# A new order of the calls on all engines in a fused mixture and three transformer blocks, and another last reader of one bank

## What is computed

```python
x_norm = modulate(_ln(x), shift_a, scale_a)
q, k, v = split(x_norm @ W_qkv + b_qkv)               # 16 heads of 16
attn_w = softmax(einsum('bhqd,bhkd->bhqk', q, k) * scale)
x = x + gate_a * (heads(attn_w @ v) @ W_proj + b_proj)
q_c = _ln(x) @ W_qc + b_qc
k_c, v_c = split(_ln(context) @ W_kvc + b_kvc)         # 77 context tokens
x = x + heads(softmax(q_c @ k_c * scale) @ v_c) @ W_cproj + b_cproj
h = gelu(modulate(_ln(x), shift_m, scale_m) @ W_mlp1 + b_mlp1)   # 1024 wide
x = x + gate_m * (h @ W_mlp2 + b_mlp2)
```

## Time and profile before

| | |
|---|---|
| median of 3 runs | 2887.1 us |
| the profiled execution | 2888.95 us, span 2887.1 us |
| busy: TensorE, VectorE, ScalarE, GpSimd | 94%, 64%, 54%, 33% |
| mean granted clock of TensorE | 0.974 |
| TensorE busy, 850 to 2810 us | 1873.45 of 1960 us |
| spread of the reciprocals, first to last unit | 733 to 2814 us, 47 units' distance |

### The profile page before, as it was taken

How to read it: one execution, slowest core, us unless ns; L and a number is a source line. 1 busy time by engine, 2 the same in 40 slices (tenths; PEclk the granted TensorE clock), 3 DMA queues, 4 the chain that set the end, 5 groups by cost and what they waited for, 6 DMA issues and landing times.

```text
span 2887.1 us, 64022 instructions
## 1 busy us (share of the span) xinstructions
PE 2716.0 (94%) x24276; PEld 2292.3 (79%) x24276; DVE 1834.0 (64%) x3776; ACT 1554.4 (54%) x2715; POOL 949.1 (33%) x963
## 2 busy tenths in 40 slices
PE   7999999994899999999999999999999999999998
PEld 6999999993577777777777777777777778778776
DVE  2444444434667777777677777777676676776753
ACT  3444444432365656655555566556555665665653
POOL 3444444321123333333232332332333223333223
PEclk9999999996799999999999999999999999999998
DMA  5123222105244453454455544434445445445331
GB/s 158 63 93 102 90 82 91 51 9 159 66 101 98 102 120 91 101 115 104 121 121 134 115 92 109 117 88 108 120 108 145 117 105 115 92 103 109 90 79 42
DMA packets 280418, 290.63 MB, mean 101 GB/s; under 512 B 90736, under 2 KB 206816, under 8 KB 280112
## 3 DMA queue, kind: packets, MB, share of 16 engines
q1 hardware_dynamic: 268656, 259.65, 36.7%
q10 hardware_dynamic: 11456, 26.88, 3.0%
HBM read 105.33 MB, written 35.85 MB: 49 GB/s over the span
## 4 chain that ended last, share of the span: by engine, by line
PE 58%; DVE 6%; issue 5%; POOL 2%; DMA 2%; SPq 2%; ACT 1%; ACTq 0%; POOLq 0%; DVEq 0%
PE gbank L3394 9%; PE obank L3234 8%; PE obank L3241 6%; PE gbank L3234 6%; PE obank L3319 5%; PE score L3299 4%; PE obank L3365 3%; PE score L3285 3%; DVE m_a L2596 2%; PE score L3348 2%; PE gbank L3249 2%; PE gbank L3334 2%; PE obank L3334 2%; PE gbank L3225 2%; PE obank L3468 1%
## 5 line engine op out<-in xcount | busy, mean ns | idle before, releaser
L2049 ACT ACTIVATE p_f<-score 128x1024 f32<-128x1024 f32 (+1 forms) x576 | 566.9, 1022 | 243.2 <-PE score L3299 219.3
L2596 DVE TENSOR_REDUCE m_a<-score 128x4 f32<-128x1024 f32 x384 | 459.4, 1218 | 132.6 <-PE score L3285 132.3
L1897 POOL TENSOR_TENSOR h_c<-h_f,h_c 128x512 fp32r<-128x512 f32 x192 | 246.4, 1284 | 640.5 <-DVE h_c L2670 640.5
L3394 PE MATMUL gbank<-w_down,h_c 128*128 128x256 f32 x2304 | 336.5, 294 | 1.2 <-POOL h_c L1897 1.2
L3394 PEld LDWEIGHTS gbank<-w_down,h_c 128*128 128x128 f32 x2304 | 292.4, 190 | 16.0 <-POOL h_c L1897 1.6
L1153 PE MATMUL m_ps<-m_comb,m_w 128*128 128x256 f32 x2304 | 295.4, 284 | 1.5 <-PEq L253 1.5
L1153 PEld LDWEIGHTS m_ps<-m_comb,m_w 128*128 128x128 f32 x2304 | 279.9, 188 | 5.0 <-issue 3.6
L2606 DVE TENSOR_REDUCE m_b<-gbank 128x4 f32<-128x308 f32 x192 | 92.1, 480 | 224.5 <-PE gbank L3334 191.7
L768 POOL TENSOR_TENSOR m_hhl<-m_hf,m_hhl 128x512 fp32r<-128x512 f32 x96 | 125.1, 1303 | 267.2 <-DVE m_hhl L992 267.2
L3319 PE MATMUL obank<-p_f,v_s 128*20 128x256 f32 x3072 | 204.2, 396 | 0.5 <-ACT p_f L2049 0.4
L3299 PE MATMUL score<-q_cat,k_cat 50*128 50x256 f32 x1536 | 190.3, 318 | 9.7 <-DMA q_cat<-mT_a 7.9
(11 more groups left out here) (289 smaller groups left out, 5613.6 us busy)
## 6 DMA issues: line engine op xcount, KB each, us to landing
q_cat<-q_hl SPq DMA_DIRECT2D x288, 128.0 KB, 3.5
k_cat<-k_hl SPq DMA_DIRECT2D x288, 128.0 KB, 3.8
qc_cat<-qc_hl SPq DMA_DIRECT2D x288, 128.0 KB, 3.1
split_L<-m_cut SPq DMA_DIRECT2D x36, 512.0 KB, 4.1
x_a<-x_after_L SPq DMA_DIRECT2D x48, 256.0 KB, 2.6
x_b<-x_after_L SPq DMA_DIRECT2D x48, 256.0 KB, 4.2
kc_cat<-kc_hl SPq DMA_DIRECT2D x288, 39.0 KB, 2.0
x_after_L<-y_c SPq DMA_DIRECT2D x32, 256.0 KB, 2.4
```

The source lines that it names most:

```text
L1897: e.tensor_tensor(h_c[:, 1, 2 * i:2 * i + 2, :], h_f[:, i % 2, :, :], h_c[:, 0, 2 * i:2 * i + 2, :].bitcast(F32), ALU.subtract).then_inc(S ...
L2049: e.activation(p_f[i % 4][0:n, :], score[i % 2].ap[0:n, :, :].rearrange("p h n -> p (h n)"), ACT.Exp, scale=SCALE).then_inc(ex.sem, 1)
L2596: e.tensor_reduce(m_a[:, :, i::NPAIR].rearrange("p t h -> p h t"), score[i % 2].ap[:, :, :].rearrange("p h (t k) -> p h t k", t=TT), AX.X, ...
L3394: mm = e.matmul(B_DOWN.ap[:, tt, :], h_c[:, xp, 2 * i + c, tt * P:(tt + 1) * P], W["down"][:, i, wp, c, :], start=(i + wp + xp + c == 0), ...
```

## The change

1. All five lists of calls are put in another order. Each list holds the same calls as before; the start and the end that are written out become longer (the loops run over n = 10 to 41, 11 to 41 or 11 to 42 instead of 5, 6 or 7 to 44 or 46). The `next_...` calls outside of the loops, where they did nothing, are gone.
2. On VectorE `cross_values_out` comes ahead of `cross_keys_low`. The bank that both read is given back by the later of them, so the wait in `cross_keys_values` that leaves the signal changes.

```diff
@@ cross_keys_values
                 e.wait_ge(*S["K_cT"].at(a))
-                turn(B_KV, S["K_vs"], a)
+                turn(B_KV, S["K_kl"], a)
```

The loop of TensorE after, from the reciprocals on, one turn (indices as in the loop over n):

```diff
+                self_recips_spread(n - 3)
+                cross_keys_values(n - 3)
+                self_projected(n - 3)
+                up(n - 5, 2)
+                self_plain(n - 2, 7)
...
+                self_turned(n - 2)
+                up(n - 6, 3)
+                self_max_rows(n - 3)
+                cross_turned(n - 4)
+                keys(n - 2)
+                cross_queries(n - 4)
+                cross_recips_spread(n - 5)
+                queries(n - 2)
+                self_scores(n - 3, 0)
+                self_scores(n - 3, 1)
+                down(n - 6, 0)
+                down(n - 6, 1)
+                down(n - 6, 2)
+                cross_projected(n - 5)
+                down(n - 6, 3)
+                self_scores(n - 3, 2)
+                self_scores(n - 3, 3)
+                cross_plain(n - 4, 0, 0)
+                cross_plain(n - 4, 0, 1)
+                self_values(n - 3, 0)
...
+                cross_plain(n - 4, 2, 1)
+                down(n - 6, 4)
+                self_scores(n - 3, 6)
+                cross_plain(n - 4, 3, 0)
+                cross_plain(n - 4, 3, 1)
+                self_scores(n - 3, 7)
+                down(n - 6, 5)
+                down(n - 6, 6)
+                down(n - 6, 7)
+                cross_max_rows(n - 4)
+                self_plain(n - 2, 0)
+                self_plain(n - 2, 1)
+                mlp_turned(n - 5)
+                self_values(n - 3, 2)
+                self_values(n - 3, 3)
+                cross_scores(n - 4, 0)
+                cross_scores(n - 4, 1)
+                values(n - 2, 0)
+                values(n - 2, 1)
```

The loop of VectorE after, whole turn:

```diff
+                self_x_high(n - 2)
+                self_x_low(n - 2)
+                context_stats(n - 3)
+                self_max_low(n - 3)
+                cross_x_low(n - 4)
+                mlp_h_high(n - 6, 2)
+                cross_queries_low(n - 4)
+                keys_low(n - 2)
+                mlp_h_high(n - 6, 3)
+                cross_heads_normed(n - 5)
+                self_stats(n - 1)
+                queries_low(n - 2)
+                context_normed(n - 3)
+                cross_sum(n - 5)
...
+                mlp_normed(n - 5)
+                self_normed(n - 1)
+                mlp_gated(n - 6)
+                cross_max_low(n - 4)
+                self_max(n - 2, 0)
+                self_max(n - 2, 1)
+                mlp_x_high(n - 5)
+                values_out(n - 2)
+                mlp_x_low(n - 5)
+                self_recips(n - 3)
...
+                self_max(n - 2, 5)
+                self_heads_normed(n - 3)
+                cross_recips(n - 4)
+                self_max(n - 2, 6)
+                cross_values_out(n - 3)
+                cross_keys_low(n - 3)
+                mlp_h_high(n - 5, 1)
+                self_sum(n - 3)
+                cross_stats(n - 3)
...
+                self_max(n - 2, 7)
+                cross_normed(n - 3)
```

GpSimd, the whole turn (before: self_rstd, mlp_sum, self_residual, mlp_h_low 0 and 1, self_out_gated, mlp_residual, cross_rstd, mlp_h_low 2 and 3, cross_residual, context_rstd, mlp_rstd), and the part of SyncE's turn behind the cross maxima:

```diff
+                self_rstd(n)
+                mlp_rstd(n - 4)
+                cross_residual(n - 3)
+                mlp_sum(n - 5)
+                self_residual(n - 2)
+                mlp_h_low(n - 4, 0)
...
+                mlp_h_low(n - 4, 1)
+                cross_rstd(n - 2)
+                context_rstd(n - 1)
+                mlp_h_low(n - 4, 2)
+                mlp_h_low(n - 4, 3)
+                self_out_gated(n - 1)
+                mlp_residual(n - 4)
...
                 sums_out(n - 2, s_a, u_a, S["A_ue"], S["A_rc"], S["A_sum"])
+                recips_out(n - 2, rcat_a, r_a, S["A_rh"], S["A_rl"], S["A_rb"], S["A_rec"])
                 pack(n - 2, u_a, S["A_sum"], S["A_pack"])
-                recips_out(n - 2, rcat_a, r_a, S["A_rh"], S["A_rl"], S["A_rb"], S["A_rec"])
```

More of the change, by code:

```diff
@@ new lines, in _ @@
+            self_max(5, 0)
+            self_max(5, 1)
+            mlp_x_high(2)
+            values_out(5)
+            self_recips(4)
+            mlp_x_low(2)
+            self_max(5, 2)
+            self_normed(6)
+            self_max(5, 3)
+            self_max(5, 4)
+            self_heads_normed(4)
+            context_stats(5)
+            mlp_h_high(2, 0)
+            cross_recips(3)
+            self_max(5, 5)
+            self_max(5, 6)
+            cross_values_out(4)
+            cross_keys_low(4)
@@ new lines, in _ @@
+            self_recips(5)
+            self_max(6, 2)
+            self_max(6, 3)
+            self_max(6, 4)
+            mlp_h_high(3, 0)
+            self_heads_normed(5)
+            self_max(6, 5)
+            cross_recips(4)
+            cross_values_out(5)
+            cross_keys_low(5)
+            mlp_h_high(3, 1)
+            self_sum(5)
+            cross_stats(5)
+            self_max(6, 6)
+            self_max(6, 7)
+            cross_normed(5)
+            self_x_high(7)
+            self_x_low(7)
@@ new lines, in _ @@
+            mlp_gated(4)
+            cross_max_low(6)
+            self_max(8, 0)
+            self_max(8, 1)
+            mlp_x_high(5)
+            values_out(8)
+            self_normed(9)
+            mlp_x_low(5)
+            self_recips(7)
+            self_max(8, 2)
+            self_max(8, 3)
+            self_max(8, 4)
+            mlp_h_high(5, 0)
+            self_max(8, 5)
+            self_heads_normed(7)
+            cross_recips(6)
+            self_max(8, 6)
+            cross_values_out(7)
@@ new lines, in _ @@
+            self_max(41, 2)
+            context_stats(41)
+            self_normed(42)
+            self_max(41, 3)
+            self_max(41, 4)
+            mlp_h_high(38, 0)
+            cross_recips(39)
+            self_heads_normed(40)
+            cross_values_out(40)
+            cross_keys_low(40)
+            mlp_h_high(38, 1)
+            cross_stats(40)
+            self_max(41, 5)
+            self_max(41, 6)
+            self_sum(40)
+            self_max(41, 7)
+            self_x_high(42)
@@ new lines, in _ @@
+            cross_max_low(42)
+            mlp_gated(40)
+            cross_stats(42)
+            self_max(44, 0)
+            self_max(44, 1)
+            mlp_x_high(41)
+            self_normed(45)
+            self_recips(43)
+            mlp_x_low(41)
+            values_out(44)
+            self_max(44, 2)
+            mlp_h_high(41, 0)
+            self_max(44, 3)
+            self_max(44, 4)
+            self_heads_normed(43)
+            self_max(44, 5)
+            mlp_h_high(41, 1)
+            cross_recips(42)
@@ new lines, in _ @@
+            up(1, 2)
+            self_plain(4, 7)
+            self_turned(5)
+            up(1, 3)
+            cross_turned(3)
+            self_max_rows(4)
+            keys(5)
+            cross_queries(3)
+            cross_recips_spread(2)
+            self_scores(4, 0)
+            self_scores(4, 1)
+            queries(5)
+            down(1, 0)
+            down(1, 1)
+            cross_projected(2)
+            down(1, 2)
+            down(1, 3)
+            self_scores(4, 2)
+            cross_plain(3, 0, 0)
@@ new lines, in _ @@
+            down(1, 6)
+            cross_max_rows(3)
+            down(1, 7)
+            self_values(4, 2)
+            self_plain(5, 0)
+            self_plain(5, 1)
+            mlp_turned(2)
+            self_values(4, 3)
+            cross_scores(3, 0)
+            values(5, 0)
+            context_turned(4)
+            cross_scores(3, 1)
+            cross_scores(3, 2)
+            values(5, 1)
+            cross_values(3, 0)
+            cross_values(3, 1)
+            cross_scores(3, 3)
@@ L3883, in _ @@
             cross_plain(45, 0, 1)
[L3884 removed]
+            down(43, 4)
             cross_plain(45, 1, 0)
```

2418 lines of the change are left out of this document (1886 added, 532 removed).

## The result

The kernel after takes 2845.32 us (median of 4 runs, 2843.27 to 2848.92), the kernel before 2891.97 beside it (4 runs): a ratio of 0.9843 [0.9812, 0.9874], 46.6 us less. The prediction was 2854, made as 33 us less than 2887.1. The profiled execution of after has a span of 2841.5 us against 2887.1.

A forecast was written before the change was run, and what follows sets the result against it. TensorE's own stream was taken as the bound, busy 94% of the span. Gains of 22 (xn_b), 10 (shapes), 4 (m_a) and 6 (start) less 9 for new waits made 33 us off 2887.1: 2854 us, 8-in-10 range 2816 to 2888.

The forecast's parts named there:

- The signs that I named: xn_b waits under 5 us, its operations 0.4 us with none at 1.4, units 42.5 to 43.0 us, h_f waits still 24.
- the xn_b term: TensorE's wait for the cross normalisation, shortened by VectorE's shorter chain and GpSimd idle beside the pair: 22.1 us gain, lower bound 0.
- the start: First units: earlier self_stats(1), self_normed(1) and weight loads, later context statistics; 6 us gain booked, bounds 0 and 12.
- the shapes: TensorE's loop: one change of matmul group shape less per unit, 0.22 us each; 10 us gain, bounds 0 and 16.
- the new waits: Cross maxima's rows landing about when cross_scores 0 is due: 0.2 us in 46 units, 9 us charged, bounds 0 and 30.
- m_a: TensorE's 7.4 us wait on the row maxima, self_normed moved beside the downs: 4 us gain, bounds -10 and +7.4.
- The plain scores: TensorE's 18.6 us wait for the last q and k rows: no change, 0 booked, bounds -15 and +10.
- Rival A: Late maxima's rows and cross queries' rows cost 0.8 us a unit, eating the gain: 2882 us; chance 0.11.
- Rival B: Packs for self_heads_normed land too late, margin 0.7 us, stopping self_projected: slower, 2923 at 2.2 us late; 0.12 with other slower ends.
- Rival C: Cross normalisation stays late, pair colliding again or self_sum slipping 0.35 us: 22 us not gained, 2876 us; chance 0.09.
- D: More is won: no new wait, start 12 instead of 6, plain scores' 18.6 us wait gone: 2820 us; chance 0.20.
- The margin of cross_queries_low: On VectorE, now first in queue, it may delay keys_low, h_high 3 and cross_heads_normed by 0.5 us at most.

The follow-up runs named there:

- b_two_edits: Kernel before with two VectorE moves: mlp_h_high 2 behind context_stats, next unit's self_stats and self_normed among the cross maxima; 2843.89 us, 0.9842 of before.
- b_high2_later: Kernel before with one VectorE call moved: mlp_h_high 2 behind context_stats instead of ahead of cross_normed; 2859.97 us, 0.9899 of before.
- a_start_back2: Kernel after with first_of_the_rest put back behind self_max_high(0), self_stats(1) and self_normed(1) behind both low parts of unit 0; 2857.19 us, 0.9898 of before.
- after_again: The kernel after, unchanged, measured again beside the kernel before; 2846.39 us, 0.9846 of before.
- b_rstd_first: Kernel before with one GpSimd call moved: cross_rstd ahead of self_out_gated and mlp_residual; 2969.63 us, 1.0268 of before.

## Why the prediction was right, and where its terms were off

The direction, the range and the cause hold: TensorE waited for xn_b because GpSimd held VectorE up, and after the change it doesn't. The signs that I named came: 0.3 us of waits on xn_b, no operation on it of the long kind, 22.2 us on h_f, and a unit of 42.38 or 42.57 us where I had 42.5 to 43.0. The forecast was 9 us too high, and the gain 14 us larger than the 33 booked, as the kernel before was itself 5 us slower beside the kernel after than the 2887.1 that I started from. That the total came so near is in part luck: the xn_b term and the start were counted too low, the shapes too high and the new waits too low, and these errors partly cancel. The parts of the profiled spans, by the spreads of the reciprocals (first spread; units 0 to 3, 4 to 30, 31 to 43, 44 to 46; the rest):

| | first | 0-3 | 4-30 | 31-43 | 44-46 | rest | span |
|---|---|---|---|---|---|---|---|
| before | 733.5 | 183.3 | 1197.6 | 566.7 | 132.6 | 73.4 | 2887.1 |
| after | 722.2 | 183.7 | 1166.1 | 562.3 | 131.1 | 76.1 | 2841.5 |
| b_two_edits | 735.8 | 181.4 | 1166.4 | 554.8 | 132.1 | 73.3 | 2843.8 |

- **xn_b, 22 us booked.** Mechanism right, price too low: the move alone gave 29 to 33, above what I had called the upper bound. I took the wait as the profile lists it, 22.1 us. But cross_turned came 0.84 us later than after the change (1.05 behind self_max_rows against 0.21), of which the row shows 0.67 as idle; the rest is inside the group. The keys behind it took 0.20 us more from signal to signal, waiting for the low part of x behind the long pair. And layer 3, which has no xn_b at all, gained too: in b_high2_later A went from 12.13 to 11.62 there. That is a third collision, which I had not seen: in layer 3 the cast of x_a, its high part, stood beside mlp_h_low 2 and took 0.94 us (the median of 14, from 2167 us on) where it takes 0.43 in b_high2_later. The difference of 0.51 us is that of A. Of the steps that I named, two had no share: cross_values_out out of the chain is worth nothing, and cross_rstd ahead is by itself a large loss. That the second is harmless in the kernel after goes with mlp_h_low 2, self_out_gated and mlp_residual standing elsewhere there; no run tests it.
- **m_a, 4 us booked.** The move alone gave 5, not clear of nothing, and behind the first 9 to 16, so the term was probably too small, by up to 12. I had read the 1.6 us of self_normed in front of self_max 0 and took it for its own time. It is the second collision of the same kind. One look at all the lengths of L2558, tile by tile, would have shown it.
- **Shapes, 10 us booked.** The price of 0.22 us was measured as 0.31 and 0.22, and C is 0.11 us shorter in after than in b_two_edits. But B holds the three `down` together and is not shorter than in before (17.68 against 17.69): a new wait on the cross queries' rows stands in it. The price is right or a little low; the 10 us that the regrouping was to give in all do not show.
- **The plain scores, 0 booked.** 18.6 us became 5.3, and 8.7 came in at cross_plain. Both wait for the same series of 18 transfers behind cross_queries. Through B the two cancel, so 0 was right for B, for a reason that I had only in part.
- **The start, 6 us booked.** 11.3 us sooner at the first spread, but units 0 to 3 take as long as before and the end 2.7 us more. Of the 11.3 the moves of VectorE and ScalarE that a_start_back2 puts back are worth about half.
- **New waits, 9 us charged.** In the list they are 8.7 us at cross_plain, 6.8 at the self scores on the maxima's rows and 4.2 at the cross scores on theirs, where the same places had 1.2, 1.3 and 2.8 before: 14.4 more. Rival A in a small form.
- **Rival B** didn't come: in the unit shown the last pack lands 41.9 us after the spread and self_heads_normed starts at 43.0. The median of that margin over units 4 to 30 is 1.6 us, in after_again 1.0, where I counted 0.7. TensorE's wait on oT_a is 3.6 us in two places. **Rival C** fell with the pair at 0.74, and D had the right mechanism in the start and the plain scores, but not the right terms.
- The margin of cross_queries_low was enough: mlp_h_high 3 and cross_heads_normed behind it delayed nobody, and `down` waited for qc_hl 1.6 us in all.

That two moves equal the whole change is the main finding. The rest of the change gives 13.6 us at the start and, by the medians, 0.3 to 0.5 us in a unit, and loses it again: in single long units between 4 and 30 (unit 17 took 50.6 us), so that the sum there is that of b_two_edits, in units 31 to 43 (7.5 us more), in units 0 to 3 and at the end (5 together). For unit 17 the trace of after shows how. TensorE waited 2.17 us for the cross queries' rows, which cross_plain now wants sooner, in a stretch where the DMA engines were busy 0.98 of the time (1485 to 1496 us). Then the granted clock stood at 1.2 GHz from 1496.0 to 1506.3 us (0.51), and a lone `down` took 1.65 us there instead of 0.97. Of the eight profiles of after and its variants six have 3.4 to 17.1 us at this level in unit 17, of the six of before and its variants only b_rstd_first (3.4). So the new order seems to bring these falls; no run was made to test it. What else belongs to the order and what differs from run to run was not settled: after_again has 1162.5 and 566.4 us for the two middle parts. Whether b_two_edits with the start of the kernel after would be faster than both was not tried.

## What to carry to other kernels

List all the durations of one operation over the whole trace: two lengths for the same shape, 0.4 and 1.35 us, were here the sign that another engine held it up, and what to move is the call that sets the other engine off, not the operation that waits. Price a wait by when its user comes, not by the idle time beside its name: of the 1.04 us that late xn_b cost cross_turned and the keys here, the idle time showed 0.67. And test the smallest edit first, since here two moves on one list, three calls in all, gave as much as five reordered lists.

## What was not expected of the hardware

VectorE's cast is held up as its tensor_scalar is: 1.55 us instead of 0.42 beside GpSimd's long operations. So is the TENSOR_TENSOR that makes the low part of x_a from two tiles in SBUF, in the two units of layer 3 of before where it meets one: 1.65 us instead of 0.69. Meanwhile the row maxima (TENSOR_REDUCE, 1.19 to 1.22 us) and the sum read from PSUM (0.68 us) keep their time beside the same operations. Three VectorE instructions in a row can each be held for one GpSimd operation, so that engine's work put together in a block, behind the rstd, cost 77 us here, part of it through the granted clock, which fell to 1.2 GHz behind the longer waits. One more change of shape in TensorE's stream costs 0.22 to 0.31 us, whether the lone group is a `down` or a half of values.
